# PV of four heads in one piece in every fourth step, and the copy of the raw outputs two steps earlier

## The reference

```
q, k, v = x Wq + bq, (x Wl + bl) Wk + bk, (x Wl + bl) Wv + bv     # 16 heads of 8, latent of 32
x1  = layernorm(x + softmax(q k' / sqrt(8)) v Wo + bo)            # for each of 16 sequences
S   = sigmoid(x1 Wg)                                              # 8 experts
each expert takes its 1024 best tokens, gelu(t W1 + b1) W2 + b2, times S, added up by token
out = layernorm(x1 + sum)
```

## Time and profile before

| | us |
|---|---|
| median of 3 runs | 573.29 (572.45 to 573.41) |
| the profiled execution, its own time | 575.32 |
| its span, first to last instruction | 573.6 |
| attention's main part, first PV to the last transpose L902 | 33.57 to 275.98 |
| the end of attention, up to norm of the last sequence | 275.98 to 285.8 |
| what follows | 285.8 to 573.6 |

### The profile page before, as it was taken

The page is one execution under the profiler, slowest core; times in us unless marked ns, Lnnn a source line. Parts: engine busy times, 40 slices in busy tenths (PEclk is TensorE's granted clock), DMA queues, the critical chain, the costliest instruction groups (busy, mean ns, idle before and its releaser), DMA issues. The chain is left out here.

```text
span 573.6 us, 9967 instructions
## 1 busy us (share of the span) xinstructions
PE 421.4 (73%) x3382; PEld 320.2 (56%) x3383; DVE 318.6 (56%) x877; ACT 263.8 (46%) x551; POOL 289.1 (50%) x379
## 2 busy tenths in 40 slices
PE   5899999999999999999810157999564839392000
PEld 4677776677766676767510134899454829381000
DVE  4577676867667676787369796344222404221025
ACT  3176776767777677677700044543212304040007
POOL 9350436333243534311330057788878888777720
PEclk9999999999999999999955555899868878697555
DMA  3322123332313232230401002244525434243353
GB/s 88 74 63 74 48 59 104 86 85 67 86 52 73 67 89 63 74 78 21 114 19 37 1 6 49 57 83 76 74 48 79 65 61 57 48 38 27 32 160 147
DMA packets 44247, 37.72 MB, mean 66 GB/s; under 512 B 6216, under 2 KB 37992, under 8 KB 44200
## 3 DMA queue, kind: packets, MB, share of 16 engines
q1 hardware_dynamic: 32488, 28.18, 18.2%
q0 software_dynamic: 11264, 8.66, 11.9%
q10 hardware_dynamic: 448, 0.28, 0.2%
HBM read 13.57 MB, written 10.62 MB: 42 GB/s over the span
## 5 line engine op out<-in xcount | busy, mean ns | idle before, releaser
L1201 DVE TENSOR_REDUCE row_max<-banks 128x2 f32<-128x512 f32 x256 | 167.6, 680 | 53.9 <-PE banks L973 52.8
L780 ACT ACTIVATE probs<-banks 128x512 f32<-128x512 f32 x256 | 140.5, 596 | 45.2 <-PE banks L993 42.7
L973 PE MATMUL banks<-k_pad,q_stack 96*128 96x256 f32 x512 | 121.5, 322 | 1.9 <-DMA k_pad<-k_lo 1.9
L672 POOL DMA_INDIRECT summed<-v_flat,to_index x64 | 101.1, 1580 | 23.9 <-issue 20.6
L993 PE MATMUL banks<-q_stack,k_pad 100*128 100x256 f32 (+3 forms) x512 | 102.5, 283 | 0.0
L973 PEld LDWEIGHTS banks<-k_pad,q_stack 96*128 96x128 f32 x512 | 82.1, 197 | 20.4 <-issue 17.2
L825 ACT ACTIVATE hT_flat<-banks,b_cols 128x512 f32<-128x512 f32 x64 | 42.6, 688 | 108.3 <-PE banks L1115 107.3
L1010 PE MATMUL banks<-probs,v_flat 128*32 128x256 f32 x1024 | 81.6, 391 | 0.9
L993 PEld LDWEIGHTS banks<-q_stack,k_pad 100*128 100x128 f32 (+3 forms) x512 | 79.1, 190 | 1.6 <-issue 0.8
L658 POOL DMA_INDIRECT v_flat<-x_table,from_index x64 | 64.0, 1000 | 24.5 <-issue 23.9
L596 POOL TENSOR_SCALAR inverse<-neg_lg 128x16 f32<-128x16 f32 x16 | 4.3, 269 | 123.3 <-ACT neg_lg L772 120.4
(11 more groups left out here) (204 smaller groups left out, 609.5 us busy)
## 6 DMA issues: line engine op xcount, KB each, us to landing
q_stack<-q_hi SPq DMA_DIRECT2D x32, 128.0 KB, 3.1
w_buf<-in_L_ffn_W SPq DMA_DIRECT2D x16, 256.0 KB, 3.2
k_pad<-k_hi SPq DMA_DIRECT2D x60, 64.0 KB
x_table<-rows SPq DMA_DIRECT2D x16, 136.0 KB, 2.4
rows<-in_L_attn_x SPq DMA_DIRECT2D x8, 256.0 KB, 2.9
q_stack<-q_lo SPq DMA_DIRECT2D x16, 128.0 KB, 3.3
summed<-rows SPq DMA_DIRECT2D x16, 128.0 KB, 2.8
hT_flat<-summed SPq DMA_DIRECT2D x4, 512.0 KB, 5.4
```

Of the source, the lines that this page charges most:

```text
L672: g.indirect_dma_start(summed, bass.IndirectOffsetOnAxis(ap=to_index[:, side, c:c + 1], axis=0), y_out[:, side, c], None, compute_op=ALU.a ...
L780: s.activation(probs[:, h % 8], ps_second[:, h % 2], ACT.Exp, scale=SCALE).then_inc(exp_done, 1)
L973: mm = t_.matmul(ps_first[:, h % 3, i * SEQ:(i + 1) * SEQ], q_stack[0:ROWS_1, n % 2, side, t, i * P:(i + 1) * P], k_pad[0:ROWS_1, n % 2, c ...
L1201: v.tensor_reduce(row_max[:, c, 2 * t:2 * t + 2], ps_first[:, h % 3].rearrange("p (i j) -> p i j", i=2), AX, ALU.max).then_inc(first_free, 1)
```

## The change

Four numbers in the table of steps: the second half of a group's PV goes from step 4g + 19 to step 4g + 17, right behind the first half, and `copy_o` of a sequence goes from step 16b + 32 to step 16b + 30.

```diff
@@ -54,7 +54,7 @@
 V_STEP = (14, 16)
 TAIL_STEP = {"norm": 34, "oT": 38, "y": 40}
 STATS_STEP, AVERAGE_STEP = 42, 43
-PV_STEP, O_STEP, POWER_STEP, GATE_STEP = (LAG + 5, LAG + 7), 32, 56, 62
+PV_STEP, O_STEP, POWER_STEP, GATE_STEP = (LAG + 5, LAG + 5), 30, 56, 62
 LAST_STEP = (BATCHES - 1) * HEADS + AVERAGE_STEP
 LATE_GATES = {1: BATCHES - 2, 4: BATCHES - 1}
```

## The result

The changed kernel took 570.03 us (median of 5 runs, 568.22 to 570.60) against 573.41 (572.45 to 573.95) of the kernel before in the same timing: ratio 0.9935, 95% interval 0.9916 to 0.9955, so 2.6 to 4.8 us less. The forecast was 564.6 us, a gain of 8.7. Ratios compare fast runs alone; one run of all, 709.07 us of the kernel before with xT in the other bank, was a slow one.

What follows compares the result with a forecast made beforehand. PE's own instructions were taken to bound attention, with some waits for ACT. Savings of 9.8 us in 59 cycles less 0.9 at the end gave 8.9, rounded to 8.7: 564.6 us for the median, range 560.5 to 570.

Steps and rivals of the forecast that it cites:

- What bounds it: From first PV to last transpose L902, PE's own instructions are the time: busy 241.66 of 242.41 us.
- The price of a piece: Second half of PV right behind the first: costs PE 0.43 us, against 0.66 or 0.76 for a half by itself.
- No wait; 0.23 saved: Cycles whose third head's step has a job: it holds PE longer than ACT's 0.13 wait; 0.23 us saved each.
- My check of DVE: DVE's four maxima need 2.5 of 3.35 us, three banks lie between it and PE: no wait.
- ACT holds PE up in the cycles with jobs too: Rival, or late shift_t rows: 0.15 in 33 cycles, gain only 1.5 to 5 us, 568 to 572; 16%.
- The forecast's own sign of being wrong: Wrong if no wait for L780 shows, PE waits for DVE, or PV's fours are more than 0.24 us apart.
- The wait for ACT: Plain cycles, third pair L993: waits for first exponential plus 0.05 hand-over; loss 0.23, net saving 0.10 us.
- The extra 0.10 of the first product behind a PV: First product after a job or PV: 0.10 us, taken as paid for the job anyway, so not saved.
- The cycles with v: Cycles with copy and v: 0.23 + 0.17 - 0.01 = 0.39 us saved in each of 6.
- The copy: Raw outputs' copy ahead of first exponential: net -0.05 us in 8 cycles without v; 0.17 wait goes in cycles with v.
- The end of attention: After first passes run out (step 256): about 0.9 us given back, 0.3 of it in the cycle from 272.81.
- The clock: Rival: PE idling 0.2 to 0.4 us in about 30 cycles halves the granted clock; six such cycles give 576 us; 6%.

Runs made afterwards that it cites:

- the control in the kernel before: xT written into job bank 0 in place of 1, in the kernel before: 573.27 us, ratio 0.9988 (0.9973 to 1.0003).

## Why the prediction was wrong

- **What bounds it**: right. PE was full, its work fell, and the time followed where no other wait appeared.
- **The price of a piece**: right. 0.43 us for the second half inside a piece, read at one place at the very end of attention, held throughout (1.00 from PV to L902 in place of 0.57).
- **"No wait; 0.23 saved" in the cycles with a job**: this step failed. I asked only whether the job is long enough to hide ACT's exponential, and not what the job itself waits for. It holds PE for 0.56 us in six cycles (3.4 us). Everything needed was in the kernel and the trace of before: every job first waits until its bank is free (`last_free` in `run_job`), the bank is freed by `scale_o` (L1237) behind the maxima on DVE, and the trace shows the weight load of L921 waiting for L1237 six times. The rows above give 0.56 us. My check of DVE went by its rate (2.5 of 3.35 us) and by the three banks of the first pass; a rate says nothing of one instruction at its place. Of the rival "ACT holds PE up in the cycles with jobs too", the size (gain 1.5 to 5) came true, the mechanism did not: it was DVE. The forecast's own sign of being wrong, PE waits for DVE, is what came. Two edits that take the wait away in different ways show it (xT in the other bank, o_nat ahead of the maxima), and so does the control in the kernel before.
- **The wait for ACT**: the mechanism was right, and it was placed in the right cycles; the hand-over was mis-sized. 0.05 us was read at one place, at the end of attention. In the stretch it is 0.11 to 0.12, which makes 0.06 to 0.07 in 25 cycles, 1.7 us. It was to be had from the cycle of the earlier trace rows too, where the copy ends at 230.64 and the PV that waits for it loads its weights 0.12 later:

```profile
230.76 0.19 PEld L1010 LDWEIGHTS banks<-probs,v_flat 128*32 128x32 f32 x8 [0.28 <-issue]
```

- **The extra 0.10 of the first product behind a PV**: wrong in the other direction, +1.4 us, as the 14 cycles with y show. In the cycle with k, whose job has two products of 512 columns, nothing of it is seen; why is open.
- **The cycles with v**: 4.18 for a forecast of 4.16 is in part luck. A wait for ACT of at least 0.14, which the forecast put at 0.01, is hidden by a saving that it did not have; that this is the 0.10 of the job behind L993 fits, but no run shows it for v.
- **The copy**: right to 0.06. Its gain in the cycles with v and its loss in the others cancel.
- **The first PV**: left out. Its second half has moved up into a cycle that no half has left, 0.43 us.
- **The end of attention**: forecast -0.9, and right. The last cycle went from 3.17 to 3.49, 0.3 us. From the last L902 to the last norm (L940) it took 9.83 us and takes 10.43, 0.6 us; with the order of before it is 9.83 to 9.85 in all three traces with whole exponentials, with the changed order 10.42 or 10.43 in all eight. Behind it, up to L1033, the order is the same in all, and the time goes with the granted clock: 5.99 us at 0.88 after the change, 6.15 at 0.74 before it, 6.49 at 0.70 and 7.25 at 0.50 in two other traces. Why the clock differs there is open.
- **The clock**: the rival did not happen. Granted clock 1.00 with PE busy for 230.31 of 235.93 us, and 1.00 in the end with 8.07 of 9.86. Waits of 0.3 to 0.6 us in about 30 of 59 cycles left the clock at full speed. The Trainium skill (TensorE: Matmul & The Clock Gate, A second HAM failure mode) tells of a kernel that cycled through PSUM banks and whose short idles between groups of products made the clock go to and fro; the traces of this case do not show that. The price of this rival was also added up wrongly: six cycles of 3.4 us more are 20 us, so from 564.6 the time would be 585 and not 576.
- **The sum**: 1.7 us too little wait for ACT and 1.6 too little gain with y, bound and b1 cancelled by luck; the 3.4 of norm and xT and the 0.4 of the first PV did not. The chances were too sure: the range had no room for a wait of a kind that I had not listed.

## What to carry to other kernels

When a piece of work is moved away from between two others, ask of every instruction behind the gap what it waits for, with the reader's place in its own engine's order; that an engine has time to spare is no answer. A long piece of work without waits was a cover for everything behind it, and in its place a job of another kind can serve: put the small jobs where PE would wait. Read the price of a hand-over between engines in more than one place, and check each new order for two jobs that meet in one buffer.

## What the runs showed of the hardware

- From the end of an activation to the weight load of the PE instruction that waits for it, 0.12 us in the stretch (170.53 to 170.65 after the change, 230.64 to 230.76 before it), and at the end of attention 0.05 (283.89 to 283.94) or 0.10 (282.11 to 282.21). Why they differ is open. From the end of a DVE instruction it is 0.06 (145.93 to 145.99).
- Products in strips of 32 columns, in fours, follow at 0.22 us (0.43 for two fours), and the entry and the way out cost about 0.1 each (0.33 in place of 0.24 from L993 to the first four, 0.33 in place of 0.22 behind the last). The weights of the job's product behind them are not loaded ahead (L948 at 153.43), and the job takes 0.48 us in place of the 0.37 behind L993, where they are (149.70).
- An exponential of 512 columns takes 0.60 us and one of 256 columns 0.38 (166.97 in the run with half of the exponential).
